# The last head group taken back half first: a new order for an attention stage on one core

## The reference, cut to what matters

```python
scores = jnp.einsum('bnth,bnsh->bnts', q, k) * (1.0 / math.sqrt(h))
scores = jnp.where(causal, scores, -jnp.inf)
attn = jax.nn.softmax(scores, axis=-1)
out = jnp.einsum('bnts,bnsh->bnth', attn, v)
```

## Time and profile before

| | us |
|---|---|
| median of 3 runs | 843.52 (843.07 to 843.75) |
| the profiled execution, own time | 847.18 |
| its span, first to last instruction | 845.5 |
| PE busy in the span | 783.0 (93%) |
| DVE busy | 621.9 (74%) |
| ACT busy | 439.2 (52%) |
| POOL busy | 305.9 (36%) |

### The profile page before, as it was taken

The page is one execution under the profiler, slowest core; times in us unless marked ns, Lnnn a source line. Parts: engine busy times, 40 slices in busy tenths (PEclk is TensorE's granted clock), DMA queues, the critical chain, the costliest instruction groups (busy, mean ns, idle before and its releaser), DMA issues.

```text
span 845.5 us, 18993 instructions
## 1 busy us (share of the span) xinstructions
PE 783.0 (93%) x7930; PEld 368.7 (44%) x7930; DVE 621.9 (74%) x881; ACT 439.2 (52%) x594; POOL 305.9 (36%) x233
## 2 busy tenths in 40 slices
PE   8669787886999999999999999999988999999997
PEld 2434444443544444444333444444424544444444
DVE  3998999998556333446659999999966787774344
ACT  4976667564854330133227788778895533332100
POOL 0698798994103000148501233222243122221000
PEclk9597999999999999999999999999999999999999
DMA  6900000005221000019900000000051033310001
GB/s 218 380 4 2 3 3 3 3 4 172 103 72 47 0 1 1 1 35 198 165 2 2 2 3 2 2 2 2 5 180 61 1 104 123 125 73 0 13 38 50
DMA packets 53296, 46.62 MB, mean 55 GB/s; under 512 B 38289, under 2 KB 44241, under 8 KB 53218
## 3 DMA queue, kind: packets, MB, share of 16 engines
q1 hardware_dynamic: 53218, 45.49, 18.6%
HBM read 34.87 MB, written 2.16 MB: 44 GB/s over the span
## 4 chain that ended last, share of the span: by engine, by line
PE 69%; DVE 16%; issue 5%; ACT 5%; POOL 2%; DMA 1%; SPq 1%; DVEq 0%; ACTq 0%; POOLq 0%
PE ps L906 13%; PE ps L670 10%; PE ps L647 9%; PE ps L828 8%; DVE arena L1458 7%; PE ps L942 7%; PE ps L726 6%; PE ps L749 6%; PE ps L805 4%; DVE arena L1684 2%; PE ps L561 2%; PE ps L753 2%; PE ps L515 1%; POOL arena L1294 1%; ACT arena L1195 1%
## 5 line engine op out<-in xcount | busy, mean ns | idle before, releaser
L1684 DVE TENSOR_REDUCE arena<-ps 128x1 f16<-128x512 f32 (+3 forms) x320 | 183.3, 630 | 16.5 <-PE ps L749 8.3
L1195 ACT ACTIVATE arena<-ps 128x1024 f32<-128x1024 f32 (+2 forms) x160 | 143.6, 942 | 36.7 <-PE ps L805 33.8
L1294 POOL TENSOR_TENSOR arena<-arena 128x1024 f32<-128x1024 f32 x62 | 145.8, 2381 | 16.6 <-DVE arena L1458 12.1
L1458 DVE TENSOR_TENSOR_SCAN arena<-arena,ps 128x1024 f32<-128x1024 f32 x64 | 142.4, 2270 | 5.5 <-ACT arena L1038 3.0
L906 PE MATMUL ps<-arena 128*128 128x512 f16 x528 | 114.6, 379 | 0.1
L670 PE MATMUL ps<-arena 128*128 128x512 f16 (+1 forms) x464 | 97.6, 372 | 1.0 <-ACT arena L1115 1.0
L749 PE MATMUL ps<-arena 64*128 64x512 f16 (+3 forms) x384 | 91.6, 329 | 3.3 <-DVE arena L1684 1.3
L561 PE MATMUL ps<-arena 64*128 64x64 f16 x3072 | 60.3, 196 | 33.2 <-DVE arena L1458 30.0
L561 PEld LDWEIGHTS ps<-arena 64*128 64x128 f16 x3072 | 52.5, 99 | 85.2 <-DVE arena L1458 72.1
L647 PE MATMUL ps<-arena 128*128 128x512 f16 x384 | 88.9, 384 | 0.0
L1038 ACT ACTIVATE arena<-arena,negA 128x1024 f32<-128x1024 f32 x64 | 72.4, 1145 | 28.1 <-DVE arena L1458 26.9
(11 more groups left out here) (180 smaller groups left out, 965.5 us busy)
## 6 DMA issues: line engine op xcount, KB each, us to landing
arena<-in_w_q_dram SPq DMA_DIRECT2D x11, 768.0 KB, 4.1
arena<-c_rows SPq DMA_DIRECT2D x16, 512.0 KB, 11.0
arena<-in_w_s_dram SPq DMA_DIRECT2D x11, 384.0 KB, 4.9
arena<-in_x_fm_dram SPq DMA_DIRECT2D x8, 256.0 KB, 4.2
out_dram<-arena SPq DMA_DIRECT2D x8, 256.0 KB, 2.0
arena<-in_wg_dram SPq DMA_DIRECT2D x1, 1792.0 KB, 9.9
arena<-in_wu_dram SPq DMA_DIRECT2D x1, 1792.0 KB, 7.2
arena<-in_wd_dram SPq DMA_DIRECT2D x1, 1792.0 KB, 11.2
```

Of the source, the lines that this page charges most:

```text
L1195: nc.scalar.activation(dst, src, ACT.Exp, scale=float(HD) ** -0.5).then_inc(exp_done, 1)
L1294: nc.gpsimd.tensor_tensor(hC[i % 4][:], hst[i % 3][:], c_all[:, n, :], ALU.mult).then_inc(hc_done, 1)
L1458: nc.vector.tensor_tensor_scan(hst[i % 3][:], dA[i % 3][:], banks(2 * (i % 2), 2), 0.0, ALU.mult, ALU.add).then_inc(scan_done, 1)
L1684: nc.vector.reduce_max(maxima_slot(half, k), ps[:, ring_bank(n), 0:len(heads) * w].rearrange("p (a w) -> p a w", a=len(heads)), AX, negate ...
```

## The change

The order string is new for the whole stage. In the last group the pairs come as (7,1), (7,0) instead of (7,0), (7,1): searches, turns, keys, values, divides and the final out follow this order. `HALVES` lists the pairs in their new order, and `PLACE`, a pair's position in it, takes the place of `2 * g + half` in all counts. A third `m_neg` buffer holds the maxima of (7,1), whose searches now follow those of (6,1) directly. SP's weight loads stay ahead of the rows of (7,1), now the last but one pair. The load of tile 1's scales waits for the end of group 6 as before. POOL's multiplication of tile 0 by its scales moves from behind the mask of (7,0,3) to behind that of (7,1,4). In the string x stands ahead of the 12 searches of (7,0), y behind their turn, and z late among the values.

```diff
-        m_neg = [view(199.5 + h / 8, 4 * GH, f16).rearrange("p (i a) -> p i a", i=4) for h in range(2)]
+        m_neg = [view(199.5 + h / 16, 4 * GH, f16).rearrange("p (i a) -> p i a", i=4) for h in range(3)]
...
+        def turned_maxima(g, half):
+
+            return m_neg[2 if (g, half) == (NG - 1, 1) else half]
+
...
-        STEPS = [(g, half, j) for g in range(NG) for half in range(2) for j in range(4 * half + 4)]
+        HALVES = [(g, half) for g in range(NG - 1) for half in range(2)] + [(NG - 1, 1), (NG - 1, 0)]
+        PLACE = {at: n for n, at in enumerate(HALVES)}
+        STEPS = [(g, half, j) for g, half in HALVES for j in range(4 * half + 4)]
...
-                     "ssksvvsksdkssvvskskssvsskksvskssvskskssvtskkssvsksksssksnskdssvskskssvvtksskssvsskkdssvtsskksvv"
...
-                     "snkdsvskstvskssvksskssvksskdvsskskssvvsksksvssksvtksksvskssksvkssvsskksssvkkdnssssksvvtsksskskss"
-                     "svksskdsvsksvvskksssvksskvsksskvssksvtksskssskkssvskskdssvkvkntvkkvkkdxvvkvkkvkkvkvkkkyzvkkkvvvv"
...
+                     "ksssksksvvtskssksssvsksksvskssvssvkkssvskskssvkssksvtdsdkssvsskksvsksksssknskvtsksvkssvskskssvsk"
+                     "ssksvksksvsksssvskkssvsskskvsksskvkndtdkvkvkkxvvkdsssksvksskvskssskvksskvktkyvkkvkkvdkvzkvkkvvvv"
                      "do")
...
             if j != 4 * half + 3 or (g, half) == (0, 0):
                 return None
-            return (g, 0) if half else (g - 1, 1)
+            return HALVES[PLACE[g, half] - 1]
...
-            for g in range(NG):
-                for half in range(2):
-                    if g == NG - 1 and half == 1:
-                        sp.dma_start(shift_sb[:], shifts).then_inc(ld_shift, 16)
-                        sp.wait_ge(v_ringed, NG)
-                        load_tile(0, 0)
-                        load_words(1, 1)
-                    if g or half:
-                        put_rows(g, half)
-            sp.wait_ge(pv_step, STEP_AT[NG - 1, 0, 0])
+            for n, (g, half) in enumerate(HALVES):
+                if n == len(HALVES) - 2:
+                    sp.dma_start(shift_sb[:], shifts).then_inc(ld_shift, 16)
+                    sp.wait_ge(v_ringed, NG)
+                    load_tile(0, 0)
+                    load_words(1, 1)
+                if n:
+                    put_rows(g, half)
+            sp.wait_ge(pv_step, STEP_AT[NG - 1, 1, 0])
...
-                if at[0] == 3 and g == NG - 1:
+                if (g, half, at[0]) == (NG - 1, 1, 4):
                     pool.wait_ge(w1_full, 1)
                     nc.gpsimd.tensor_tensor(w_full[:], w_full[:], w_scales[0][:], ALU.mult).then_inc(w1_scaled, 1)
```

More of the change, by code:

```diff
@@ L260, in out_beside, with before @@
                 return None
-            return (g, 0) if half else (g - 1, 1)
+            return HALVES[PLACE[g, half] - 1]
+        def before(g, half):
+            return PLACE[g - 1, half] + 1
         OUTS = 2 * NG - 1
@@ L266, in attention_order @@
             groups = range(NG)
-            halves = [(g, half) for g in groups for half in range(2)]
             streams = {
-                "k": iter([("keys", g, half, j, u) for g, half in halves for j in range(4 * half + 4) for u in exp_units(half, j)]),
-                "v": iter([("values", g, half, j) for g, half in halves for j in range(4 * half + 4)]),
-                "s": iter([("search", g, half, k) for g, half in halves for k in range(len(SEARCH[half]))
+                "k": iter([("keys", g, half, j, u) for g, half in HALVES for j in range(4 * half + 4) for u in exp_units(half, j)]),
+                "v": iter([("values", g, half, j) for g, half in HALVES for j in range(4 * half + 4)]),
+                "s": iter([("search", g, half, k) for g, half in HALVES for k in range(len(SEARCH[half]))
                            if g or (half, k) not in EARLY_UNITS]),
                 "n": iter([("negate", g, 1) for g in groups]),
-                "t": iter([("turn", g, half) for g, half in halves if g or half]),
-                "d": iter([("divide", n // 2, n % 2) for n in range(OUTS)]),
-                "o": iter([("out", NG - 1, 1)]),
+                "t": iter([("turn", g, half) for g, half in HALVES if g or half]),
+                "d": iter([("divide", g, half) for g, half in HALVES[:-1]]),
+                "o": iter([("out", *HALVES[-1])]),
                 "x": iter([("weights", 0, 0)]), "y": iter([("weights", 1, 0)]), "z": iter([("weights", 2, 0)])}
@@ L762, in turn_maxima @@
                 for i in range(4):
-                    last = nc.tensor.transpose(dst[0:GH, i * P:(i + 1) * P], m_neg[half][:, i, :], ident_h[:])
+                    last = nc.tensor.transpose(dst[0:GH, i * P:(i + 1) * P], turned_maxima(g, half)[:, i, :], ident_h[:])
                 last.then_inc(ring_full, 1)
@@ L832, in turn_out @@
             def turn_out(g, half, n):
[L833 removed]
+                pe.wait_ge(o_kept, PLACE[g, half] + 1)
                 bank = ring_slot(n)
@@ L1696, in early @@
                 else:
-                    maxima(*EARLY_UNITS[n], n)
+                    maxima(0, *EARLY_UNITS[n], n)
             for t in range(TT):
@@ L1712, in negate @@
                 dve.wait_ge(ring_read, searched(g, half))
-                nc.vector.tensor_tensor(m_neg[half][:], m_neg[half][:], m_b[:], ALU.min).then_inc(m_joined, 1)
+                nc.vector.tensor_tensor(turned_maxima(g, half)[:], turned_maxima(g, half)[:], m_b[:], ALU.min).then_inc(m_joined, 1)
             def invert(g, half):
-                dve.wait_ge(o_copied, 2 * g + half + 1)
+                dve.wait_ge(o_copied, PLACE[g, half] + 1)
                 if g:
-                    dve.wait_ge(o_divided, 2 * g + half - 1)
+                    dve.wait_ge(o_divided, before(g, half))
                 src = o_copy[half].rearrange("p (i a d) -> p i a d", i=4, a=GH)
@@ L1760, in _ @@
                 if kind == "search":
-                    maxima(half, *at, RING_AT[kind, g, half, *at])
+                    maxima(g, half, *at, RING_AT[kind, g, half, *at])
                 elif kind == "negate":
```

28 lines of the change are left out of this document (14 added, 14 removed).

## The result

| | before | after |
|---|---|---|
| median, us (6 runs each) | 843.63 (842.81 to 845.68) | 849.0 (846.79 to 852.92) |
| ratio | | 1.0061, interval 1.0044 to 1.0077 |
| profiled execution / span, us | 847.18 / 845.5 | 852.92 / 851.2 |

The change makes the kernel 0.6 % slower, 2 us beyond the upper end of the forecast's range for 8 in 10 (847.0). Lines of the code stand eight further on than before (L1743 is now L1751, L1352 is L1360, L1195 is L1203).

A forecast was written before the change was run, and what follows sets the result against it. DVE's maxima, closely with PE, were taken to bound the kernel up to the last search, ACT's exponentials behind it. The terms gave +1.0 us, all at the tail, on a median of 843.52: 844.5 us, 8-in-10 range 841.2 to 847.0.

The forecast's parts named there:

- Step 1: Searches 1 to 268: the last ends at 608.8 us instead of about 609.3; spacing taken as 0.
- my bound of -3.3: Searches 1 to 268: lower bound for the new spacing, with DVE's wait gone, -3.3 us.
- The 0.1 us for each pair of neighbouring matmuls: Searches 1 to 268: neighbouring 64-row matmuls on the same half are 62 where 71 were, saving perhaps 0.9 us.
- My count of long PE runs: Searches 1 to 268: PE runs over about 1.25 us between searches are 8 where 3 were, at most 3 us.
- rival (b): Searches 1 to 268: five more long PE runs leave DVE waiting, +3 us, 847.5 in all; chance 0.23.
- the cover: Beside x: ACT and PE have ten exponentials to do meanwhile, hiding delays; if it fails, up to +1.5 us.
- Step 2: Turn of (7,1): first keys 3.77 us after the last search, at 612.6; PE not idle, cost 0.
- step 3: ACT up to unit (7,1,4): ten exponentials, a copy and about 0.8 us of waiting, ending at 624.1; no stall.
- step 5: x ahead of the searches of (7,0): 3.7 us of DVE, up to 2.4 more from group 6's masks and divides.
- Step 4: End of attention: DVE's weights and POOL's masks alternate behind the scaling; last o_raw copy at 638.85, +1.35, taken as +1.0.
- the 0.35 that I then took off: End of attention: +1.35 us lowered to +1.0, as no row showed a mask stopping y's two-operand passes.
- Rival (a): End of attention: the tail really shortens, ACT sets the end, copy 2.3 to 2.8 us earlier, 841.0; chance 0.25.

The follow-up runs named there:

- e5: Kernel before with the new string up to search 240 and the old order, (7,0) ahead of (7,1), behind it: 842.83 us, ratio 0.9991.
- e0: The changed kernel measured again with no edit: 848.97 us, ratio 1.0063 to the kernel before.
- e1: Changed kernel with the divides of (5,0) and (5,1) moved some 16 and 10 exponential units earlier, as in the order before: 846.11 us, ratio 1.0019.
- e7: Changed kernel with DVE's nibble, unscale, y and z passes on the first two weight tiles cut to one eighth of their columns: 840.67 us, one execution.
- e2: Changed kernel with y moved behind the reciprocal of (6,1), so POOL's divide of (6,1) need not wait for y: 844.97 us, ratio 1.0012.
- e3: Changed kernel with the second half of z, a 1.76 us pass, moved behind DVE's last division: 846.61 us, ratio 1.0024.
- e6: Changed kernel with 28 spare 128x512 matmuls, results never read, put where PE stood idle: 845.78 us, ratio 1.0022.
- e8: Kernel before with DVE's passes on the first two weight tiles cut to one eighth of their columns: 844.88 us, one execution.
- e12: Changed kernel with the two early divides, POOL's scaling behind the mask of (6,1,7), and 11 spare matmuls in PE's gaps: 842.12 us, ratio 0.9980.
- e9: Changed kernel with the two early divides and POOL's scaling behind the mask of (6,1,7) instead of (7,1,4): 844.13 us, ratio 0.9993.

## Why the prediction was wrong

**Step 1 was right.** Search 268 ended at 608.29 us where 608.8 was predicted. DVE's waits for PE's searches from 440 to 608 are small:

```profile
606.40 1.89 DVE L1692 TENSOR_REDUCE arena<-ps 128x1 f16<-128x512 f32 x3 [0.24 <-PE ps L761]
...
DVE arena L1692 <- PE ps L761: 1.5, 7, 0.3
...
DVE arena L1692 <- PE ps L757: 0.9, 4, 0.3
```

Their sum is 2.4 us. Before it was 6.1, the 3.3 of the earlier trace rows and a second row of the same waits, which my bound of -3.3 left out:

```profile
DVE arena L1684 <- PE ps L749: 2.8, 11, 0.4
```

Counted from the turn of (0,1), search 240 ended 0.94 us earlier than before, in the profile after and in e5 alike, so the spacing saved a little where I had put 0. The 0.1 us for each pair of neighbouring matmuls in my sum came from no row, and no run measured it. My count of long PE runs, on which rival (b) stood, decided nothing.

**Steps 2, 3 and 5 failed at one point: the cover.** Step 2 says "so nothing stands idle; cost 0", step 3 gives ACT 0.8 us of waiting in its ten exponentials, and step 5 counts on ACT and PE as cover for x. The first keys of (7,1) did come as forecast, at 611.98, 3.69 us behind the last search (3.77 predicted), but the next keys unit waited 2.32 us. ("No stall there", in step 3, is said of the keys of (7,0), and there it held.) I followed keys, exponentials, values and searches through the new string, and the divides only at the end. I had named the masks and divides of group 6 as a delay for x, with ACT and PE as cover. But two divides of group 5 had slid to this place as well, and through `o_copy` ACT, PE and the searches of (7,0) wait for them. The cover was the victim. Price: 1.67 us (16.49 to 14.82, e0 to e1), and 1.5 us of clock in the profiled execution. With them the scaling ended 2.8 us later than the 627.9 that I predicted; in e0, without the clock, 1.3 later. Step 5's price for a cover that fails, up to 1.5, would have held the second but not the first; none of it went into my sum. Step 5's own price, x beside the searches, stayed within its bound: from turn to turn e7, with x cut to an eighth, takes 0.66 us less than e1, where the pause is gone too.

**Step 4 was right in mechanism, and its total in part by luck.** From the scaling's end to the last copy I predicted 10.95 us, or 10.60 with the 0.35 that I then took off; it is 10.63. Two errors inside nearly cancel: y took 4.48 us where I had 3.88 (four masks held up all its passes, where I had let one stop it), and z 4.79 where I had 5.60 (its passes and POOL's three operations ran partly beside one another). The masks of 1 to 2 us, the stretched L1751, the reciprocal behind y that holds the divide and the last masks, and a last copy bound by POOL are all there. Where I left y's two-operand passes between two bounds, they were stopped (1.53 and 1.12 us). e2 and e3 take one of these causes away each and give 1.9 and 1.5 us back.

**A term was missing.** My sum ended at the last o_raw copy and took the 6.58 us behind it as they were. With PE waiting for masks between 636 and 642 its clock fell, and the next stage started 1.95 us later. I had read that the clock stood at 1.00 throughout and didn't ask what the longer waits of PE would do to it. By the Trainium skill ("TensorE: Matmul & The Clock Gate", Part 1) the gate passes all or half of the pulses by how busy the engine has been; the two levels in these profiles, 1.00 and 0.50, and e6 agree.

**The sum, mended:** predicted +1.0; the pause 1.67 and the clock behind it 1.5; the clock at the end 1.95; against that 0.3 for steps 1 to 5 together. That is 5.8 us, the difference of the two profiles. (The 0.3 is the remainder, not a measurement.)

**Rival (a) had the right price.** I put the shorter tail at 2.3 to 2.8 us if the weights kept out of the way; e7 against e8, with most of that work left out of both, gives 2.5. Its condition was not met, as the row with the mask of 2.08 us had said.

## What to carry to other kernels

When an order written by hand changes, follow every letter of it, the cheap ones too: here two divides of 0.6 us that free a buffer cost 1.67 us, and all the searches that moved cost nothing. Work of VectorE and GpSimd that was packed into the same stretch ran here largely behind one another (four masks of 0.63 us took 4.01 beside y), so look for a place where only one of the two is on the path. And a sum shouldn't end at the last instruction of the changed stage: longer waits of TensorE were paid a second time here, at half the clock, in the stage behind it.

## What was not expected of the hardware

The clock fell to its lower level behind a pause of 2.3 us in one execution (turn to turn 18.00 us) and not in three others of kernels with the same pause and no products in it (e0, e2 and e3: 16.48 to 16.49). What made the difference is open. At the end it fell in both profiles of the changed kernel: in the first behind three windows of 2 us with PE busy for 1.05, 0.89 and 0.50, in e0 behind 1.10, 1.49 and 0.43 (the last two and the fall are shown). 11 short matmuls in the gaps held it in e12. y's passes with one operand were stretched too: L1757 took 0.85 us in the profile after, and 0.41 in e9 behind the turn of (7,0).

```profile
634.00:636.00 2.00, 1.49 (x16) 0.37 (x16) 1.97 (x2) 0.00 (x0) 2.00 (x2) 1.00 0.00 0
636.00:638.00 2.00, 0.43 (x8) 0.19 (x8) 1.07 (x2) 0.06 (x1) 2.00 (x3) 1.00 0.00 0
638.00:640.00 2.00, 1.11 (x4) 0.71 (x4) 0.20 (x1) 1.81 (x2) 2.00 (x1) 0.60 0.04 8
...
631.71 0.85 DVE L1757 TENSOR_SCALAR arena<-arena 128x512 f16<-128x512 f32 x1
...
622.27 0.41 DVE L1757 TENSOR_SCALAR arena<-arena 128x512 f16<-128x512 f32 x1
```

The first three lines are of e0, the fourth of the profile after, the last of e9.
